# Reordering the attention visits, batching the layer-norm statistics, and giving the FFN's weight tile a second buffer

## What is computed

```python
Q, K, V = LN(x) * sign_q, LN(x) * sign_k, LN(x) * sign_v      # per head, elementwise
attn    = where(causal, sigmoid(Q K^T * scale * 4), 0)        # no softmax
x       = x + attn V
h       = LN(x)
x       = x + h W^T + bias + lora(h)                          # W is 4096 x 4096, lora rank 16
```

## Time and profile before

| what | us |
|---|---|
| median of the 2 runs shown | 13233.59 |
| the two runs | 12904.39 and 13562.79 |
| the profiled execution | 12996.26 |
| its span on the slowest core (core 1) | 12994.7 |
| spans of the eight cores | 12869.4 to 12994.7 |
| prologue, to 380 us on core 1 | 380 |
| attention, 380 to 10964 us | 10584 |
| FFN, 10964 us to the end | 2031 |

### The profile page before, as it was taken

How to read it: one execution, slowest core, us unless ns; L and a number is a source line. 1 busy time by engine, 2 the same in 40 slices (tenths; PEclk the granted TensorE clock), 3 DMA queues, 4 the chain that set the end, 5 groups by cost and what they waited for, 6 DMA issues and landing times.

```text
span 12994.7 us, 108588 instructions; the slowest of 8 cores (12869.4 to 12994.7 us)
## 1 busy us (share of the span) xinstructions
PE 7499.8 (58%) x36337; PEld 3570.7 (27%) x36337; DVE 4870.5 (37%) x7431; ACT 1798.0 (14%) x2377; POOL 107.6 (1%) x206
## 2 busy tenths in 40 slices
PE   0033326757767377323347776677757775566566
PEld 0011112323333133111123333333323332222222
DVE  2444444444444444444444444444444444101200
ACT  0122221101111111222211111111111111000000
POOL 0000000000000000000000000000000000000000
PEclk9966667878878688666668887888878887777677
DMA  9322222222222322222222222222222221222222
GB/s 107 111 98 93 100 107 65 65 80 67 64 83 61 99 71 65 97 110 88 91 88 65 65 65 78 68 65 65 65 81 63 62 62 58 72 67 62 72 61 65
DMA packets 559900, 998.58 MB, mean 77 GB/s; under 512 B 312501, under 2 KB 427205, under 8 KB 537797
## 3 DMA queue, kind: packets, MB, share of 16 engines
q1 hardware_dynamic: 542872, 907.73, 22.6%
q0 software_dynamic: 16480, 83.91, 3.3%
HBM read 907.61 MB, written 83.89 MB: 76 GB/s over the span
## 4 chain that ended last, share of the span: by engine, by line
PE 54%; DVE 18%; DMA 15%; SPq 5%; issue 4%; ACT 1%; another core or an unknown queue 1%; DVEq 1%; ACTq 0%; POOLq 0%; POOL 0%
PE pav L548 22%; PE pqk L505 20%; PE py L774 8%; DMA kfull<-xk 7%; DVE stsu L328 5%; SPq L84 5%; DMA khd<-xk 4%; DVE xb L380 4%; PE ptr L395 3%; DMA x1s<-ebuf 2%; DVE xbT L406 2%; DVE QgT L463 1%; DMA kfull<-xq 1%; DVEq L58 1%
## 5 line engine op out<-in xcount | busy, mean ns | idle before, releaser
L505 PE MATMUL pqk<-QgT,xbT 128*128 128x512 bf16 x12288 | 2684.1, 380 | 360.6 <-ACT stage L519 350.7
L548 PE MATMUL pav<-xb,attn 128*128 128x512 bf16 x12288 | 2822.9, 394 | 1.9 <-DVE attn L527 1.9
L395 PE MATMUL ptr<-ident,xb 128*128 128x128 bf16 x6144 | 748.0, 299 | 3359.4 <-DVE xb L380 3359.4
L519 ACT ACTIVATE stage<-pqk,cst 128x512 bf16<-128x512 f32 x1536 | 1057.7, 689 | 6502.4 <-PE pqk L505 5429.5
L505 PEld LDWEIGHTS pqk<-QgT,xbT 128*128 128x128 bf16 x12288 | 1205.1, 98 | 1825.0 <-issue 387.4
L527 DVE TENSOR_TENSOR attn<-stage,msk 128x512 bf16<-128x512 bf16 x1536 | 1063.0, 692 | 1632.3 <-ACT stage L519 1627.4
L548 PEld LDWEIGHTS pav<-xb,attn 128*128 128x128 bf16 x12288 | 1243.4, 102 | 1544.2 <-issue 204.4
L565 DVE SCALAR_TENSOR_TENSOR acc<-pav,acc 128x512 f32<-128x512 f32 x1408 | 973.6, 691 | 1595.1 <-PE pav L548 1595.1
L395 PEld LDWEIGHTS ptr<-ident,xb 128*128 128x128 bf16 x6144 | 572.7, 135 | 3554.7 <-issue 3554.7
L774 PE MATMUL py<-wtb,h2T 128*128 128x512 bf16 x4096 | 1037.8, 418 | 607.4 <-DMA wtb<-wb 607.4
L328 DVE TENSOR_REDUCE stsu<-kfull 128x1 f32<-128x4096 f32 x144 | 636.4, 4420 | 806.7 <-DMA kfull<-xk 679.8
(11 more groups left out here) (106 smaller groups left out, 1415.1 us busy)
## 6 DMA issues: line engine op xcount, KB each, us to landing
khd<-xk SPq DMA_DIRECT2D x640, 512.0 KB, 4.7
kfull<-xk SPq DMA_DIRECT2D x128, 2048.0 KB, 7.6
msk<-mk SPq DMA_DIRECT2D x96, 1024.0 KB, 8.8
khd<-xq SPq DMA_DIRECT2D x128, 512.0 KB, 4.3
wb<-wgt POOLq DMA_DIRECT2D x4, 8192.0 KB, 203.7
kfull<-xq SPq DMA_DIRECT2D x16, 2048.0 KB, 7.7
y<-yb POOLq DMA_DIRECT2D x128, 256.0 KB, 2.5
x1s<-ebuf POOLq DMA_DIRECT2D x64, 256.0 KB, 4.5
```

Of the source, the lines that this page charges most:

```text
L395: bf_ = (lambda E, dc=dc, xo=xb_buf, c0=st * HD, p=ps: E.transpose(ptr[p][:, 128 * dc:128 * (dc + 1)], xo[:, c0 + 128 * dc:c0 + 128 * (dc ...
L505: E.matmul(pqk[bank][:], xbT[b][:, HD * dc + 128 * sc:HD * dc + 128 * (sc + 1)], QgT[:, CH * dc + 512 * th:CH * dc + 512 * (th + 1)], star ...
L519: sgv = op("s", "S", lambda E, ss=ss, bank=bank: E.activation(out=stage[ss][:], in_=pqk[bank][:], func=AF.Sigmoid, scale=cst[:, 0:1]))
L548: E.matmul(pav[bank][:], attn[:, CH * sc + 128 * tc:CH * sc + 128 * (tc + 1)], xb[b][:, HD * sc + 512 * dh:HD * sc + 512 * (dh + 1)], star ...
```

## The change

Four things are changed. The diff, cut to its core:

```diff
@@ main loop @@
                 ttv = plan_qk_sig(q, h, k, ev_last, mdv)
+                plan_av(q, h, k, ttv)
+                if k == L - 1:
+                    plan_epilogue(sidx, q, h)
                 if fi + 1 < len(flat):
                     ...
                     prepped[fi + 1] = plan_visit_prep(nq, nh, nk, nstats)
-                plan_av(q, h, k, ttv)
-                if k == L - 1:
-                    plan_epilogue(sidx, q, h)
@@ plan_visit_prep, visits with statistics @@
+                    for st in range(NS):
+                        kfull_slot.acquire("sy")
+                        dmv = dma("sy", kfull[:], ..., sem="KR0")
+                        sv = plan_stats_reduce(kfull[:], dmv, st)
+                        W("v", *dmv)
+                        rc_ = op("v", "V", ... E.tensor_copy(
+                            xb[b][:, st * HD:(st + 1) * HD],
+                            kfull[:, h * HD:(h + 1) * HD]))
+                        kfull_slot.release([("S", sv), ("V", rc_)])
+                    plan_stats_final(sv, mcache[:, 8 * k:8 * k + 8],
+                                     rcache[:, 8 * k:8 * k + 8])
+                    for st in range(NS):
+                        av = op("v", "V", ... E.tensor_scalar(
+                            out=xb[b][:, st * HD:(st + 1) * HD],
+                            in0=xb[b][:, st * HD:(st + 1) * HD],
+                            ..., op0=OP.subtract, op1=OP.mult))
+                        ev = plan_xpose(xb[b], xbT[b], st, av)
@@ FFN @@
-            fb = FF.enter_context(nc.sbuf_tensor("fb", [128, 4096], BF16))
+            fb = [FF.enter_context(nc.sbuf_tensor(f"fb{i}", [128, 4096], BF16))
+                  for i in range(2)]
-            wtb = FF.enter_context(nc.sbuf_tensor("wtb", [128, 32 * 512], BF16))
+            wtb = [FF.enter_context(nc.sbuf_tensor(f"wtb{i}", [128, 32 * 512], BF16))
+                   for i in range(2)]
...
+                    wp = (half * 8 + os_) % 2
+                    wtt = wtb[wp]
+                    wtb_slot[wp].acquire("sy")
```

More of the change, by code:

```diff
@@ L322, in build_program, with plan_stats_reduce @@
             W("sy", "S", pro["S"])
-            def plan_stats(kr_ap, dmv, i, mcol, rcol):
-                su, sq, m2, ve, sd, r0, t1, sq2 = stt_[i]
+            def plan_stats_reduce(kr_ap, dmv, st):
                 W("v", *dmv)
-                W("v", "G", g_const)
[L328 to L341, removed]
+                opq("v", lambda E, st=st: E.reduce_sum(
+                    suc[:, st:st + 1], kr_ap, axis=AX))
+                W("s", *dmv)
+                W("s", "V", state["scr8"])
+                half = kr_ap.shape[1] // 2
+                opq("s", lambda E, hf=half, st=st: E.activation(
+                    out=sdump[:, 0:hf], in_=kr_ap[:, 0:hf], func=AF.Square,
+                    accum_out=sqa[:, st:st + 1]))
+                sv = op("s", "S", lambda E, hf=half, st=st: E.activation(
+                    out=sdump[:, 0:hf], in_=kr_ap[:, hf:2 * hf], func=AF.Square,
+                    accum_out=sqb[:, st:st + 1]))
+                return sv
@@ L356, in plan_stats @@
                     op0=OP.mult, op1=OP.add))
[L357 to L387, removed]
@@ L418, in plan_qg_prep @@
                 if h == 0:
+                    sv = None
                     for st in range(NS):
@@ L474, in plan_visit_prep @@
                 ev = None
-                for st in range(NS):
-                    col = 8 * k + st
-                    mcol = mcache[:, col:col + 1]
-                    rcol = rcache[:, col:col + 1]
-                    if vis_stats:
-                        src, full = xk_d[CH * k + 128 * st:CH * k + 128 * (st + 1), :], True
-                    else:
-                        src, full = xk_d[CH * k + 128 * st:CH * k + 128 * (st + 1),
-                                         h * HD:(h + 1) * HD], False
-                    ev = plan_sub_pipeline(src, full, h * HD, vis_stats, mcol, rcol,
-                                           xb[b], xbT[b], st)
+                if vis_stats:
+                    sv = None
+                    for st in range(NS):
+                        kfull_slot.acquire("sy")
+                        dmv = dma("sy", kfull[:],
+                                  xk_d[CH * k + 128 * st:CH * k + 128 * (st + 1), :],
+                                  sem="KR0")
+                        sv = plan_stats_reduce(kfull[:], dmv, st)
+                        W("v", *dmv)
+                        rc_ = op("v", "V", lambda E, st=st, b=b, h=h: E.tensor_copy(
+                            xb[b][:, st * HD:(st + 1) * HD],
[4 more added lines that the diff above has]
+                    for st in range(NS):
+                        av = op("v", "V", lambda E, st=st, b=b, k=k: E.tensor_scalar(
+                            out=xb[b][:, st * HD:(st + 1) * HD],
+                            in0=xb[b][:, st * HD:(st + 1) * HD],
+                            scalar1=mcache[:, 8 * k + st:8 * k + st + 1],
+                            scalar2=rcache[:, 8 * k + st:8 * k + st + 1],
+                            op0=OP.subtract, op1=OP.mult))
+                        ev = plan_xpose(xb[b], xbT[b], st, av)
+                else:
+                    for st in range(NS):
+                        ks = state["khd"] % 2
+                        state["khd"] += 1
+                        khd_slot[ks].acquire("sy")
+                        dmv = dma("sy",
+                                  khd[ks][:],
+                                  xk_d[CH * k + 128 * st:CH * k + 128 * (st + 1),
+                                       h * HD:(h + 1) * HD], sem=f"KH{ks}")
+                        W("v", *dmv)
+                        av = op("v", "V", lambda E, ks=ks, st=st, b=b, k=k:
+                                E.tensor_scalar(
+                                    out=xb[b][:, st * HD:(st + 1) * HD],
+                                    in0=khd[ks][:],
+                                    scalar1=mcache[:, 8 * k + st:8 * k + st + 1],
+                                    scalar2=rcache[:, 8 * k + st:8 * k + st + 1],
+                                    op0=OP.subtract, op1=OP.mult))
+                        khd_slot[ks].release([("V", av)])
+                        ev = plan_xpose(xb[b], xbT[b], st, av)
```

91 lines of the change are left out of this document (52 added, 39 removed).

## The result

| | before | after |
|---|---|---|
| median of all runs, us | 12923 (10 runs) | 13090 (11 runs) |
| undisturbed executions, us | 12904 to 12926 | 13008 to 13013 |
| profiled execution, us | 12996.26 | 13137.75 |

The ratio is 1.0077, with a 95% interval of 1.0051 to 1.0104. The change makes the kernel slower by 0.8%, about 100 us. The forecast was +19 us. These cores' spans are longer by 102.1 us in the mean (core 7: 12900.4 to 12994.9).

What follows compares the result with a forecast made beforehand. No engine is full; alternating stages of PE, DVE and DMA bound the kernel. Order +193, sweep changes +54, statistics -46 and -43, `fb` -46, `wtb` -93 sum to +19 on 12996: 13015 us, range 12850 to 13260.

Steps and rivals of the forecast that it cites:

- The seams: Per visit, gaps between PE's matmul blocks and transposes: 4.96 us after against 2.77 before, +2.19, over 88 visits +193 us.
- Transposes to `pav`: nothing. `pav` to `pqk`: nothing: In the old order's visit, these two joints on PE were taken to cost no time.
- `pqk` is that first block: Behind the preparation, `pqk` instead of `pav` pays about 2 us to regain full clock; `pav` then runs warm at 27.79.
- The change of sweep: At seven sweep changes the new order loses the overlap of `pqk` with the epilogue: +7.7 us each, +54 us.
- The queries' load and SP's other moved DMAs are hidden: At the epilogue, moved loads cost nothing: two `khd` buffers stay filled, two of eight rounds remain at the last load.
- The mask: Loaded behind the eighth slice, first used 13.0 us after issue; loads take 12.5 at most, so cost taken as nothing.
- The batch: Batched statistics in preparations: -2.9 us per visit, 16 visits, -46 us; for the queries -21.7, twice, -43 us.
- `fb` and `wtb`: Second buffers in the FFN: `fb` saves 46 us of DVE and PE waits, `wtb` 93 us of PE's weight waits.
- The weights become hidden: FFN rival, faster: block n+1's weights issue while block n computes, another 500 us saved, 12500 us; chance 0.05.
- The clock falls at the new seam: Rival: the 1.85 us between `pqk` and `pav` returns PE to 1.2 GHz, +185 us, 13200 us; chance 0.05.
- The loads with statistics slow down: Rival, slower: 126 `kfull` loads, closer together, each take 1.9 us more, +240, 13260 us; chance 0.05.
- The mask comes late: Rival, slower: the mask lands 2.6 us late on average, 15.6 us after issue, giving 13260 us; chance 0.03.

Runs made afterwards that it cites:

- the wait alone: Kernel before, plus one wait per preparation making PE's `pav` wait for the last copy to `xbT`; 13085 us against 12903 to 12912.
- filling the seam: Changed kernel plus eight useless 128-wide matmuls between the last transposes and the wait for `xbT`; 12914 us against 13008 to 13013.
- the order alone: Kernel before with only the new order, `pav` planned right behind `pqk` and ahead of the next preparation; 13242 and 13255 us against 12894.
- the interleaved kernel: Changed kernel with the old order back and the next weight block's 32 loads between the eight `xsl` loads; 12109 us against 12903 and 12912.
- the batch alone: Kernel before with only the batched statistics, old order and old FFN; 12794 and 12795 us against 12894.

## Why the prediction was wrong

**The seams: right.** 1.87, 1.96 and 1.12 us stand where 1.85, 2.10 and 1.01 were forecast: 4.95 in sum against 4.96.

**"Transposes to `pav`: nothing. `pav` to `pqk`: nothing": wrong by 0.37 us a visit.** Where no wait stands between two blocks of matmuls, they overlap, and the trace of before had it: the first `pqk` starts at 2997.86, while `pav` runs from 2968.53 for 29.49, to 2998.02. A joint that gets a wait loses its overlap on top of the wait. Two joints (-0.21 and -0.16) were counted as 0. So the new seams cost 4.95 + 0.37 - 2.77 = 2.55 us.

**"`pqk` is that first block" at the same 2 us: wrong by 0.6 to 0.8.** The forecast moved the cold start from `pav` to `pqk` at an even price, because both blocks have 128 matmuls of one shape. But on core 7 `pav` (29.37, +1.58) started straight behind transposes and `pqk` (29.95, +2.16) starts behind an idle 1.12 us. The forecast saw both facts, the cold block and the new seam in front of it, and priced each as if the other weren't there. That the seam is the cause is shown from both sides: the wait alone makes `pav` 0.7 us longer, and filling the seam makes `pqk` 0.8 us shorter.

Together, less 0.2 us in the transposes: 2.19 + 0.37 + 0.60 - 0.2 = 2.96, measured +2.95 on core 7. In the mean of cores 4 to 7 it is +3.13, and over 66 plain visits the 0.94 above the forecast are the first bold row of the table, 62 us of the miss.

**The change of sweep: right in kind, 7.7 us where 9.9 to 10.9 were measured.** With the visit next to it, the order alone costs 90 / 7 = 12.9 us per sweep and the forecast had 9.9. Of the missing 3.0, 0.8 is the same as in any visit. Another 2.0 are in the epilogue, from the end of `pav` to its last DVE instruction: 59.6 us before and 61.6 with the order alone (cores 4 to 7). The forecast put that change at nothing. Half of it is the fourth epilogue, 59.3 to 66.3 us. "The queries' load and SP's other moved DMAs are hidden" holds for PE; but the first row load goes out with two rounds to come, just ahead of a store, and that store took some 6 us longer. The other half isn't clear of the differences between traces. What is left (0.3 us more in the queries' transposes, 0.3 less given back by `pav`, 0.2 of lost overlap, some 0.6 less elsewhere) nearly cancels.

**The mask: right.** In after no wait of DVE's `attn` for `msk` stands in the list, with loads of 7.0, 8.8 and 12.7 us (least, median, most).

**The batch: right in sign, about 1 us a visit too small, out of two misses.** Copy 0.69, scaling 0.55 and a round of 2.68 are as forecast (the forecast's terms for the round add up to 2.68, not to its 2.66). Alone it gave -100 to -110 where -89 were forecast. The visits with statistics give -3.8 instead of -2.9 each. On cores 4, 5 and 7 the seven periods from the first sum to the eighth fall from 116.5 to 92.1 us, 3.5 each where 3.15 were forecast. The stretch from the eighth sum to the last transposes grows from 9.7 to 30.4 us, 20.7 where 19.2 were forecast, because the first scaling starts 4.7 us behind the last copy and not 3.1.

**`fb` and `wtb`: right.** -32 and -107 forecast, -31.5 and -108.1 measured. No clock was lost to the denser FFN: on cores 5 and 7, 112 of the 128 groups took 7.1 us before and 114 after, the others being those that open a block. (The 26 us that the forecast set aside for this were too few: on core 1 of before 47 groups took 7.1 us and 60 took 8.6, so all of them at the slower pace would cost some 70 us. Likewise its bounds, added up, give 12959 to 13157 and not 12930 to 13125. Nothing in the miss hangs on either.)

**The rivals.** *The weights become hidden* did not happen in this change, and did once SP's list was changed too: -545 us, about the 500 that the rival priced. The Trainium skill's page "Trainium Kernel Development and Optimization", section Best Practices, names double-buffering as what overlaps DMA with compute; here the buffer was the smaller part of it, and the order of issue the larger. *The clock falls at the new seam* did not: `pav` is at 27.81 us behind 1.87 us. *The loads with statistics slow down* did not: the median landing of `kfull` is 7.6 us, against 7.7. *The mask comes late* did not.

The forecast's time, 13015, is near the 13008 to 13013 of undisturbed executions only because it was counted from a profiled execution that was itself 70 to 92 us above the 12904 to 12926 of the others (its die 0 took 12937.5 to 12994.7, its die 1 12869.4 to 12900.4). The difference is what was to be forecast, and it was +100 and not +19.

## What to carry to other kernels

Price a reordering joint by joint: what overlapped before (a negative gap), the new wait, and what the wait does to the block behind it. On this kernel a wait of 1.0 us in front of a cold block cost 1.9. A second buffer buys only what the in-order queue in front of its load lets through: look at what stands ahead of the load in the issuing engine's list, and move that first (here 135 us for the buffers, 545 for the list). When an engine of a chain gets faster, look at what waits beside it next: the transposes sped up by useless work ended up waiting for `khd`.

## What the runs showed that was not expected

- What a block of 128 matmuls takes depends on what PE did just ahead of it: 29.2 to 29.4 us straight behind transposes, 30.1 behind the same transposes and 1.0 us of idleness, 29.2 with eight 128-wide matmuls in that idleness, 27.8 when useless matmuls had kept the granted clock at 1.00 through the preparation.
- Useless matmuls that fill waiting time made the kernel faster twice: -96 us in after, -112 to -124 us in the interleaved kernel.
- 32 transposing DMAs take 40.7 us to issue in one piece, and the same 1.25 us each (6.26 for five) when they are spread between the `xsl` loads beside full matmul work, and PE's groups keep their 7.55 us.
- The first row load of the queries, issued 0.04 us ahead of a store of 128 x 1024 bf16, goes with a wait of 9.7 to 12.3 us for that store, where some 5.2 are usual.
- The cores of one die in one execution differ by up to 50 us (13191.4 to 13240.6 with the order alone), also in stretches whose instructions no part of the change touches (plain visits with the batch alone, on core 7: -28 us over 66, on core 6: +7). A term under 30 us can't be read from one core.
